# Values moved within SBUF by sixteen DMAs from three buffers, a row shift in two DMAs, and stacks loaded per group in six DMAs

## What is computed

```python
xn = _layernorm(x, axis=-1)
x = x + _L0_attn_ref(xn, Wq, Wk, Wv, W_O) + _L0_ffn_ref(xn, Wqkv, ...)
```

```python
for i in range(DEPTH):
    x = attn_layer(shift_tokens(x), Wqkv[i], q_scale[i], k_scale[i], Wo[i]) + x
    x = ffn_layer(shift_tokens(x), ln_g[i], ln_b[i], W1[i], b1[i], W2[i], b2[i]) + x
```

## Time and profile before

| | |
|---|---|
| median of 3 runs | 2025.67 us (2023.75 to 2032.03) |
| the profiled execution | 2033.02 us, of which the span of its instructions is 2031.2 us |
| TensorE busy | 1864.3 us, 92% of the span |
| VectorE, ScalarE, GpSimd busy | 78%, 70%, 64% |
| granted TensorE clock, mean over the span | 0.962 of full speed |
| DMA queue of the program | 126816 packets, 193.87 MB, 34.9% of 16 engines |
| DMA queue of kind "instruction" (q8) | 258 packets, 4.23 MB |

### The profile page before, as it was taken

One profiled execution on the slowest core, in us unless ns is written; L12 is line 12 of the kernel. 1 busy time (PEld: TensorE's weight loads), 2 busy tenths in 40 slices (PEclk: granted clock), 3 DMA queues, 4 the chain that ended last, 5 costly groups with the idle time before them and its releaser, 6 DMA issues.

```text
span 2031.2 us, 73684 instructions
## 1 busy us (share of the span) xinstructions
PE 1864.3 (92%) x32776; PEld 1253.0 (62%) x32776; DVE 1591.5 (78%) x1819; ACT 1415.4 (70%) x2038; POOL 1305.3 (64%) x1277
## 2 busy tenths in 40 slices
PE   3989997799999999999999999999989999999985
PEld 1434443466676767666776677666766766667674
DVE  5877771798898789887987798788868987888772
ACT  1266566677777787777777777787768777777763
POOL 1011112898877797777877787778768877777630
PEclk7699999799999999999999999999999999999997
DMA  3042100254343434434343443344343443333331
GB/s 103 32 136 64 47 25 22 72 126 107 95 119 106 120 98 124 110 108 117 101 121 106 111 126 88 96 126 130 99 106 98 124 119 105 92 103 85 98 99 45
DMA packets 127132, 198.58 MB, mean 98 GB/s; under 512 B 31576, under 2 KB 56412, under 8 KB 126048
## 3 DMA queue, kind: packets, MB, share of 16 engines
q1 hardware_dynamic: 126816, 193.87, 34.9%
HBM read 134.84 MB, written 55.77 MB: 94 GB/s over the span
## 4 chain that ended last, share of the span: by engine, by line
PE 48%; DVE 21%; ACT 15%; issue 10%; POOL 5%; DMA 1%; SPq 0%; DVEq 0%; ACTq 0%; POOLq 0%
PE banks L488 8%; PE banks L497 5%; PE banks L555 4%; PE banks L582 4%; PE banks L528 4%; PE banks L565 4%; DVE arena L646 4%; PE banks L425 3%; DVE arena L763 3%; PE banks L592 3%; PE banks L515 3%; PE banks L536 3%; ACT arena L953 3%; DVE sm_t L757 3%; ACT arena L1026 2%
## 5 line engine op out<-in xcount | busy, mean ns | idle before, releaser
L1175 POOL TENSOR_TENSOR arena<-arena 128x1024 f32<-128x1024 f32 x192 | 499.1, 2624 | 0.0
L1167 POOL TENSOR_TENSOR arena<-arena,tab_sl 128x512 f32<-128x512 f32 x384 | 414.3, 1112 | 15.7 <-ACT arena L953 8.2
L488 PE MATMUL banks<-w_qkv,arena 128*128 128x512 f32 x768 | 358.7, 610 | 10.1 <-ACT arena L936 5.5
L784 DVE TENSOR_TENSOR arena<-banks,tab_cl 128x1024 f32<-128x1024 f32 x192 | 232.7, 1221 | 100.7 <-ACT arena L953 100.5
L1138 POOL TENSOR_SCALAR ss<-ss 128x32 f32<-128x32 f32 x96 | 69.2, 721 | 284.5 <-ACT rn L943 281.8
L743 DVE TENSOR_TENSOR arena<-arena,rn 128x1024 f32<-128x1024 f32 x192 | 244.1, 1311 | 0.0
L488 PEld LDWEIGHTS banks<-w_qkv,arena 128*128 128x128 f32 x768 | 139.5, 191 | 161.0 <-issue 143.8
L953 ACT COPY arena<-banks 128x1024 f32<-128x1024 f32 x192 | 192.0, 1004 | 63.7 <-PE banks L488 63.1
L646 DVE TENSOR_REDUCE arena<-banks 128x1 f32<-128x512 f32 (+3 forms) x352 | 183.2, 585 | 67.8 <-PE banks L385 58.7
L497 PE MATMUL banks<-ident,arena 128*128 128x128 f32 x1536 | 209.7, 290 | 19.9 <-issue 12.6
L893 ACT ACTIVATE arena<-banks 128x512 f32<-128x512 f32 (+2 forms) x352 | 156.5, 529 | 100.1 <-PE banks L407 89.5
(11 more groups left out here) (112 smaller groups left out, 3157.5 us busy)
## 6 DMA issues: line engine op xcount, KB each, us to landing
arena<-v_dram SPq DMA_DIRECT2D x360, 256.0 KB, 4.8
v_dram<-arena SPq DMA_DIRECT2D x96, 512.0 KB, 3.2
arena<-parts_dram SPq DMA_DIRECT2D x64, 144.0 KB
w_qkv<-Wqkv SPq DMA_DIRECT2D x6, 1024.0 KB, 5.1
arena<-v_dram SPq DMA_DIRECT2D x24, 192.0 KB, 3.3
parts_dram<-arena SPq DMA_DIRECT2D x12, 256.0 KB, 3.2
tab_cl<-tab_c SPq DMA_DIRECT2D x6, 512.0 KB, 8.0
tab_sl<-tab_s SPq DMA_DIRECT2D x6, 512.0 KB, 11.1
```

The costliest lines, as they stand in the source:

```text
L488: last = e.matmul(ps[:, BANK * c:BANK * (c + 1)], xsT[b][:, P * t:P * (t + 1)], w_qkv[:, at:at + BANK], start=True, stop=True)
L784: e.tensor_tensor(qk_rot[n % 4][:, m, :].rearrange("p (h d) -> p h d", d=HEAD_DIM), banks[:, pair_of["proj", n, m], :].rearrange("p (h d) ...
L1167: e.tensor_tensor(qk_sw[:, m, :].rearrange("p (h d) -> p h d", d=HEAD_DIM)[:, :, d:d + HALF], raw[:, m, :].rearrange("p (h d) -> p h d", d ...
L1175: e.tensor_tensor(to, to, qk_sw[:, m, :], ALU.add).then_inc(S["rs"], 1)
```

## The change

Three edits, all on SP's DMAs and on what waits for them.

1. **Values.** `v_dram` and `store_values` are gone. `windows(n)` waits for the copy of V itself and moves its rows from SBUF to SBUF: for each of the 4 windows of a tile, each of the two places (as the window itself, as the one before it) and each half of the channels one DMA of 32 partitions by 512 values (64 KB), 16 in all, 14 where a sequence begins. It stands where the store stood, a step earlier than the loads stood. V has three buffers, and `values(n)` on ScalarE waits until the window DMAs of the tiles n-3 and n-2 have landed.
2. **Row shift.** The DMA of 127 partitions is cut into one of 112 and one of 15.
3. **Stacks.** The slots of the ring lie in one piece for each of Q and K, and a group's stacks are loaded by six DMAs of 24 partitions by 4 heads by 1024, in place of eight of 72 by 1024. All six count on one semaphore for the group, where each head had its own.

```diff
-        STACK_DMAS = 2
+        STACK_DMAS = 2 * PARTS
...
-        V = [stack(INNER) for _ in range(2)]
+        V = [stack(INNER) for _ in range(3)]
...
-                        w.wait_ge(stack_in[slot], STACK_DMAS * 16 * (g // 3 + 1))
+                        w.wait_ge(stack_in[g % 3], STACK_DMAS * 16 * (g // 3 + 1))
...
-                w.wait_ge(S["v_out"], max(0, 16 * (n - 1)))
-                e.copy(V[n % 2], banks[:, pair_of["v", n], :]).then_inc(S["v_ready"], 1)
+                if n >= 3:
+                    w.wait_ge(vw_in[(n - 3) % 3], 16 * windows_loaded(n - 2, (n - 3) % 3))
+                    w.wait_ge(vw_in[(n - 2) % 3], 16 * windows_loaded(n - 1, (n - 2) % 3))
+                e.copy(V[n % 3], banks[:, pair_of["v", n], :]).then_inc(S["v_ready"], 1)
...
-                    e.dma_start(QS[slot][0:ROWS, :], q.unsqueeze(1).to_broadcast([ROWS // PARTS, PARTS, seq])).then_inc(stack_in[slot], 16)
-                    e.dma_start(KS[slot][0:ROWS, :], k.unsqueeze(0).to_broadcast([PARTS, ROWS // PARTS, seq])).then_inc(stack_in[slot], 16)
...
+                for i in range(PARTS):
+                    e.dma_start(Q_ring[i:ROWS:PARTS, slots, :], parts_dram[b, 0, heads].rearrange("h x n -> x h n")).then_inc(stack_in[g % 3], 16)
+                    e.dma_start(K_ring[lines * i:lines * (i + 1), slots, :], parts_dram[b, 1, heads].rearrange("h x n -> x h n")
+                                ).then_inc(stack_in[g % 3], 16)
...
-            def store_values(n):
-                l, b, t = of_tile(n)
-                w.wait_ge(S["v_ready"], n + 1)
-                e.dma_start(v_dram[P * t:P * (t + 1), :], V[n % 2]).then_inc(S["v_out"], 16)
-
             def windows(n):
                 l, b, t = of_tile(n)
                 w.wait_ge(S["pv"], max(0, n - 2))
-                w.wait_ge(S["v_out"], 16 * (n + 1))
+                w.wait_ge(S["v_ready"], n + 1)
                 for prior in (1, 0):
...
-                    for hp in range(2):
-                        r = 64 * hp + WINDOW * (1 - prior)
-                        e.dma_start(Vw[n % 3][r:r + WINDOW, first:WPT, :], rows[:, :, BANK * hp:BANK * (hp + 1)]).then_inc(vw_in[n % 3], 16)
+                    for i in range(WPT):
+                        if i >= prior:
+                            src = V[n % 3][WINDOW * (i - prior):WINDOW * (i - prior + 1), :]
+                        elif t:
+                            src = V[(n - 1) % 3][P - WINDOW:P, :]
+                        else:
+                            continue
+                        for hp in range(2):
+                            r = 64 * hp + WINDOW * (1 - prior)
+                            e.dma_start(Vw[n % 3][r:r + WINDOW, i, :], src[:, BANK * hp:BANK * (hp + 1)]).then_inc(vw_in[n % 3], 16)
...
-                e.dma_start(to[1:P, :, hi], xg[0:P - 1, :, hi]).then_inc(xf_in[half], 16)
+                for r0, r1 in ((0, P - 16), (P - 16, P - 1)):
+                    e.dma_start(to[r0 + 1:r1 + 1, :, hi], xg[r0:r1, :, hi]).then_inc(xf_in[half], 16)
...
-                if 0 <= s - 3 < n_tiles:
-                    windows(s - 3)
                 if 0 <= s - 2 < n_tiles:
-                    store_values(s - 2)
+                    windows(s - 2)
```

More of the change, by code:

```diff
@@ L101 @@
 tab_c tab_s halves_set zero_xs zero_xf row_in xsT xs_ready proj raw sq ss_sum floor root newton rn rc sw rs rot tk tq kt_ready qt_ready kp
-sc mx sub v_proj v_ready v_out vw_first ex sm recip p_norm pT pt pv ot wo x_attn
+sc mx sub v_proj v_ready vw_first ex sm recip p_norm pT pt pv ot wo x_attn
 xf_left f_stat f_mv f_var f_rstd xf_norm f_nT xft h gel u_one u f_out x_ff final""".split()
@@ L179, in build @@
         MAXIMA_AT, TAIL = 2, 10
-        QS = [carve("A", seq // 2).bitcast(BF16) for _ in range(RING)]
-        KS = [carve("A", seq // 2).bitcast(BF16) for _ in range(RING)]
+        Q_ring = carve("A", RING * seq // 2).bitcast(BF16).rearrange("p (r n) -> p r n", r=RING)
+        K_ring = carve("A", RING * seq // 2).bitcast(BF16).rearrange("p (r n) -> p r n", r=RING)
+        QS, KS = [[ring[:, r, :] for r in range(RING)] for ring in (Q_ring, K_ring)]
         cst = carve("A", MASKS + A_HEADS * A_DIM)
@@ L223, in build @@
         YA = qk_sq.rearrange("p m (t d) -> p (m t) d", d=P)
-        v_dram = nc.dram_tensor("v_dram", [seq, INNER], F32, kind="Internal").ap()
         xf_in = [ctx.enter_context(nc.semaphore(f"xf{i}")) for i in range(halves)]
         vw_in = [ctx.enter_context(nc.semaphore(f"vw{i}")) for i in range(3)]
-        stack_in = [ctx.enter_context(nc.semaphore(f"stack{i}")) for i in range(RING)]
+        stack_in = [ctx.enter_context(nc.semaphore(f"stack{i}")) for i in range(3)]
         rows_in = [ctx.enter_context(nc.semaphore(f"rows{i}")) for i in range(RING)]
@@ L255, in slot_of @@
             return (g * A_PER_GROUP + j) % RING
-        VW_LOADS = 4
         def windows_loaded(tile_count, i):
-            return VW_LOADS * len(range(i, tile_count, 3))
+            return sum(4 * WPT - 2 * (n % tiles == 0) for n in range(i, tile_count, 3))
         def rows_passed(G):
@@ L790, in ff_stats @@
                 half = G % halves
-                w.wait_ge(xf_in[half], 32 * (G // halves + 1))
+                w.wait_ge(xf_in[half], 48 * (G // halves + 1))
                 w.wait_ge(S["xf_left"], G + 1)
@@ L1241, in load_stacks @@
                 b = g // A_GROUPS
[L1242 to L1248, removed]
-                    e.dma_start(QS[slot][0:ROWS, :], q.unsqueeze(1).to_broadcast([ROWS // PARTS, PARTS, seq])).then_inc(stack_in[slot], 16)
-                    e.dma_start(KS[slot][0:ROWS, :], k.unsqueeze(0).to_broadcast([PARTS, ROWS // PARTS, seq])).then_inc(stack_in[slot], 16)
+                h, slot = g % A_GROUPS * A_PER_GROUP, slot_of(g, 0)
+                heads, slots, lines = slice(h, h + A_PER_GROUP), slice(slot, slot + A_PER_GROUP), ROWS // PARTS
+                w.wait_ge(S["a_wsc"], max(0, 2 * (g - 2) * UNITS))
+                w.wait_ge(S["parts0_out"], PARTS * 16 * (b + 1))
+                w.wait_ge(S["parts1_out"], PARTS * 16 * (b + 1))
+                for i in range(PARTS):
+                    e.dma_start(Q_ring[i:ROWS:PARTS, slots, :], parts_dram[b, 0, heads].rearrange("h x n -> x h n")).then_inc(stack_in[g % 3], 16)
+                    e.dma_start(K_ring[lines * i:lines * (i + 1), slots, :], parts_dram[b, 1, heads].rearrange("h x n -> x h n")
+                                ).then_inc(stack_in[g % 3], 16)
             def store_parts(b):
@@ L1324, in windows @@
                 w.wait_ge(S["pv"], max(0, n - 2))
-                w.wait_ge(S["v_out"], 16 * (n + 1))
+                w.wait_ge(S["v_ready"], n + 1)
                 for prior in (1, 0):
-                    first = int(t == 0 and prior == 1)
-                    rows = v_dram[P * t + WINDOW * (first - prior):P * (t + 1) - WINDOW * prior, :].rearrange("(i r) c -> r i c", r=WINDOW)
-                    for hp in range(2):
-                        r = 64 * hp + WINDOW * (1 - prior)
-                        e.dma_start(Vw[n % 3][r:r + WINDOW, first:WPT, :], rows[:, :, BANK * hp:BANK * (hp + 1)]).then_inc(vw_in[n % 3], 16)
+                    for i in range(WPT):
[8 more added lines that the diff above has]
+                            e.dma_start(Vw[n % 3][r:r + WINDOW, i, :], src[:, BANK * hp:BANK * (hp + 1)]).then_inc(vw_in[n % 3], 16)
             w.wait_ge(S["ya_out"], 16 * batches)
```

## The result

| | before | after |
|---|---|---|
| median of 4 runs each, taken in turns | 2028.85 us (2023.75 to 2032.56) | 2005.65 us (2002.66 to 2008.89) |
| the profiled execution, its span | 2033.02, 2031.2 us | 2008.89, 2007.1 us |
| granted TensorE clock, mean | 0.962 | 0.969 |

The account below looks back on a forecast made before the run. It took TensorE to run dry when its program waits behind window-load bursts. Gains of 18 us (values) and 4 (stacks), less 1, make 21 us: median from 2025.67 to 2004.7, said as 2005 us, range 1996 to 2014.

Parts of the forecast that it names:

- The reading: Second part: a piece of TensorE's program waits in the DMA engines behind bursts of window loads; 28.0 us beyond the floor.
- the stalls stay: Rival, chance 0.20: stalls don't come from queueing behind window loads; only the stacks' 4 us remain, 2021.7 us.
- Values, 15 us in the groups: Second part's 21 groups: stalls in L555 and L497 assigned 18.4 of 28.0 us; 15 kept as gain.
- the 3.4 us kept back for the tables: Second part: taken off the 18.4 us because the tables are still loaded in one piece.
- The fill: Pipeline fill before 527 us, about 10 more tiles with the same bursts: 3 us gained.
- SP's cost: SP issuing the sixteen window DMAs: 0.65 us each, 10.4 us per tile against a 16.5 us step.
- The 1 us taken off for it: Value weights' load at layer ends, landing only 0.5 us early: 1 us lost over five layers.
- Row shift, worth 0: DMA after the shift holds SP 8.5 us per group; hidden before and after, but the sixteen need SP's time.
- Stacks, 4 us: First part, group 0: all stacks there at 40.1 us, VectorE 4 us ahead, second part starting 4 us sooner.
- The sum: Whole kernel: 18 us from values, 4 from stacks, less 1 for late weights, 21 us gained.
- SP becomes the bound: Rival, chance 0.09: SP's DMA cost makes the value weights late; slower, 2044 us at 1.05 us per DMA.
- The rule against: Skill's advice to coalesce small transfers, 2.0 us fixed per DMA: sixteen would be 32 us per tile, kernel far slower.

Follow-up runs that it names:

- e12: Kernel before, four window loads left whole, three 16-byte transfers put between one and the next; 2006.25 us, ratio to before 0.9910.
- e4: Kernel before with its four window loads cut into sixteen of 64 KB, still from HBM; 2000.97 us, ratio to before 0.9883.
- e1: Kernel before with the values edit alone; 2010.61 us, ratio to before 0.9920.
- e5: Changed kernel with four unread 256 KB DRAM-to-DRAM transfers added ahead of each tile's sixteen; 2052.56 us, ratio to before 1.0109.
- e7: Changed kernel with six 32-byte transfers added behind each tile's sixteen; 2115.61 us, ratio to before 1.0433.
- e9: Kernel before, window loads cut into sixteen from HBM, plus four unread 256 KB DRAM-to-DRAM transfers ahead of them per tile; 2070.68 us, ratio to before 1.0228.
- e2: Kernel before with the stacks edit alone; 2028.31 us, ratio to before 1.0018.
- e3: Kernel before with the row shift in two DMAs alone; 2029.01 us, ratio to before 1.0006.
- e10: Changed kernel with the row shift in one DMA of 127 partitions again; 2003.51 us, ratio to before 0.9893.
- e8: Changed kernel without the stacks edit; 2007.78 us, ratio to before 0.9903.
- e6: Kernel before with its four window loads cut into eight of 128 KB, still from HBM; 2008.30 us, ratio to before 0.9907.

## Why the prediction held, step by step

**The reading: right.** The stalls inside L555 and L497 go when the window loads no longer stand in the DMA engines together (e12, e4, e1). That it is a piece of TensorE's program that comes late behind them can be counted in the traces. Take TensorE's instructions in the order of their starts, matmuls, weight loads and semaphore instructions together (66138 of them in before), and count them off in 256s. Between 400 and 1950 us TensorE stands idle for "issue" for over 0.3 us at a time 31 times before and 12 times after, and every one of these 43 falls at place 193 or 194 of the 256. In all fourteen traces it is 236 of 242, at places 193 to 195; the other six are waits of L488 for late weights in e5, e7 and e9. The idle times of TensorE in before that another engine or a DMA ended lie all over: 67 of them at 56 different places. So TensorE stalls at the borders between pieces of 256 instructions and nowhere else; the prediction's 254 to a packet left the semaphore instructions out.

Each border has its packet of the queue of kind "instruction", 258 and 258. Between 527.5 and 1944.9 us of before there are 213 borders, and TensorE stalls at 27 of them. The packet for the next piece starts 1.2 us (median) after the border in front, and no border in any of the traces is crossed sooner than 2.2 us after its packet has started. In before, 44 of the 213 packets start over 2.5 us after the border in front; after, it is 19 of 213, in e12 31 of 212 and in e4 23 of 213. In e5 it is 45 of 212 and in e9 35 of 213: the added bursts did hold packets back, but TensorE stalled for fewer of them (9 and 10, against 15 in before). The other 12 stalls of before stand behind pieces that TensorE was through in 2.2 to 5.0 us, with packets less late than that. So both count, how late the packet starts and how soon TensorE is through the piece in front. Nor do the stalls come or go because the borders moved: e1, e4 and e12 have the 66138 instructions of before and lose nearly all of the gather's stalls (0, 1.9 and 2.1 us are left of 14.7), while e2 has the 66114 of after and keeps 9.0 us of them.

In the trace of before and of after, TensorE stands still for over 1 us inside these three stages 28 times between 400 and 1950 us; ahead of the end of each, one such packet starts 2.2 to 3.0 us earlier. For the stall of 4.35 us that ends at 940.89, the queues of before up to 937.9 us, and from there to the end of the stall:

```profile
q1 hardware_dynamic: 2514, 1.49, 67.7%
```
```profile
q1 hardware_dynamic: 351, 0.59, 93.6%
q8 instruction: 1, 0.02, 3.2%
```

From 929 to 937.9 us no packet of q8 starts; one starts in the last 3 us of the stall, 4.8 us after the border in front (933.17 us). The Trainium skill, "Runtime: NRT & Kernel Launch", instruction fetch mechanics, calls such crossings mostly hidden: at 186 of the 213 borders they are, at 27 they are not. With this count and e12 the rival "the stalls stay" falls.

**Values, 15 us in the groups: right in kind, too small.** Measured 23.2. Two parts of the term failed. First, the 3.4 us kept back for the tables: after, SP issues this layer's two tables at 933.9 and 934.3 us, in the period that begins at 922.43, and neither this pair nor the three others in the 21 groups falls in a long one: without window loads beside them they cost nothing here. Second, I gave L515's stalls their share (13.4 of 39.0) of the 28.0 us and left it. They did stay, 11.2 us, but only 4.9 us of excess is left, and 4.8 of it lies in the two long periods: short idle times in the scores hardly lengthen a period, so L555's and L497's had, by that, cost nearly all of it. **The fill**: 3 foreseen, 2.2 measured.

**SP's cost: in bounds, the mean a little higher.** The line after, and sixteen with the weights behind them:

```profile
L1331 SPq DMA_DIRECT2D arena<-arena x1512: 507/591/3897, 376.1 to 1941.4; - x189
```
```profile
576.20 40.55 SPq L1331 DMA_DIRECT2D arena<-arena  x48
616.79 0.58 SPq L1226 DMA_DIRECT2D w_qkv<-Wqkv  x1
```

Over most tiles the sixteen take 11 to 12 us, 0.73 each (the 40.55 us above hold three tiles and SP's waits for V between them), where I took 0.65 and 10.4 us. V is copied at 605.8, `load_v` issued at 616.79, L526 starts at 622.38 without a wait:

```profile
620.35 2.19 PE L495 MATMUL banks<-ident,arena 128*128 128x128 f32 x16
622.38 1.88 PE L526 MATMUL banks<-w_qkv,arena 128*128 128x512 f32 x4
```

That is 5.6 us for a load that took 5.1 (5.0 to 6.2 us in the five layers; its own landing is not in this trace): on time by some 0.5 us, the margin worked out, although a DMA costs more, since 11.0 of the sixteen's time lie behind the copy and L526 comes 16.6 us behind it where it had been 16.2. The 1 us taken off for it was not lost.

**Row shift, worth 0: right**, by e3 and by e10. That the sixteen need the 8.5 us was wrong: SP's slack in that step was enough.

**Stacks, 4 us: wrong.** Their beginning came as foreseen. TensorE and VectorE where group 0 arrives, beside the earlier trace rows:

```profile
40.46 1.01 PE L383 MATMUL banks<-arena 72*128 72x512 bf16 x2 [15.19 <-DMA arena<-parts_dram]
```
```profile
41.58 22.13 DVE L644 TENSOR_REDUCE arena<-banks 128x1 f32<-128x512 f32 x44 [5.07 <-PE banks L386]
```

One wait, 40.46 for 40.1 foreseen; VectorE's run of reductions ends at 63.71 us in place of 66.12, and the first store of maxima's rows (L1261) comes at 65.61 us, 2.4 us sooner than the 68.02 of before, not 4. And much of this is chance: over all profiled executions that store comes at 64.3 to 66.0 us with the new stacks (5 kernels, mean 65.3) and at 65.1 to 68.0 with the old (9 kernels, mean 66.2), 0.9 us apart. The step "the first part ends 4 us sooner" failed. The stores that end it, for each batch one, after and then before:

```profile
L1276 SPq DMA_DIRECT2D scratch<-arena x2: 337/338/338, 237.0 to 351.3; - x2
```
```profile
L1276 SPq DMA_DIRECT2D scratch<-arena x2: 337/340/343, 240.2 to 351.3; - x2
```

3.2 us of lead at the first batch's end are none at the second's. From the one store to the other it is 111.1 or 111.2 us in twelve of the fourteen kernels, 112.5 in e12 and 114.3 after. Over all profiled executions the last store comes at 344.8 to 351.3 us with the new stacks (5 kernels, mean 348.9) and at 345.2 to 351.3 with the old (9 kernels, mean 348.2). The first part varies by 6 us by itself, and the medians of e2 and e8 show no gain. Why the second batch took 3 us longer in this execution is not settled: stretches of the lower clock fall differently in every execution (20.5 us of them between 95 and 350 us after, 13.7 before), but they don't follow the part's length from kernel to kernel.

**The sum.** 18 + 4 - 1 = 21 was 25.4 + 0 - 0 less 1.3 in the drain, 24.1 of the span: the 4 us of the stacks that didn't come were made up by values that brought more. That the total is near is partly these two errors.

**SP becomes the bound.** It didn't happen, and its price was far too low. By the rival's sum e7, at (11.7 + 4.1)/16 = 0.99 us per DMA, would lose 80 x 0.32 + 9 = 35 us; it lost 110. The rival's sum counted `load_v` alone; each lateness there also makes the loads for queries and keys late, whose reader waited up to 17.3 us at once.

**The rule against.** The fixed 2.0 us of the Trainium skill, "DMA: Bandwidth & Descriptors", stand in its section "Anatomy of one DMA — SWDGE (gpsimd) path", a fit for DMAs that GpSimd issues, where SP issues these; by that figure, sixteen one after another would be 32 us a tile, an estimate. Here 64 KB from HBM lands in 2.0 us too (e4), but the sixteen, issued 0.46 us apart (median), overlap, and cutting four loads in sixteen made the kernel faster (0.9883), against the rule to coalesce, though 64 KB lies just at the size under which the rule speaks of overhead.

## What to carry to other kernels

When TensorE stands still inside a run of matmuls without a semaphore, count its instructions: if the places are all the same in 256s, it is the program that comes late. Then look at what SP issued in the 5 to 10 us ahead: several large DMAs at once can cost more than their bytes, and spacing them out, with tiny ones in between or by cutting them, may cure it without another route. Look for the cure with the most slack left: the changed kernel and e4 take the same time, but in one the weights for the values land about 0.5 us early by the working above and in the other 12. And judge a queue that is 70% full by all that stands behind it, since lateness there adds up from load to load.

## What the runs showed of the hardware

- SP takes 11.8 us (median) to issue sixteen DMAs of 64 KB within SBUF, 0.74 each (after); 8.6 us for sixteen of 64 KB from HBM, 0.54 each (e4); 4.4 us for eight of 128 KB from HBM, 0.55 each (e6); and 4.05 us for six of 32 bytes within SBUF, 0.68 each (e7). Here the cost goes by the kind more than by the size.
- 1 MB in four DMAs between DRAM tensors keeps the DMA engines at a median share of 0.79 over 1 to 5 us behind the first issue (e9); the same amount in four window loads at 0.95 (before), in eight at 0.80 (e6).
- TensorE stalls for "issue" only at borders 256 of its instructions apart (236 of 242 idle times in fourteen traces; the other six are waits for weights), and no border is crossed sooner than 2.2 us after the start of its packet of the instruction queue. In before, that packet starts 1.2 us after the border in front (median), 6.7 us at the latest, at the stall that ends at 656.97 us.
